# A selective-scan layer: tiles of two states by 64 channels in place of two states by 128 channels side by side

## The reference

```
x1, x2 = layernorm(group_norm(x)) ;  xin = x1 @ W_in_x.T ;  z = x2 @ W_in_z.T       # 384 inner channels
for each direction (forward, backward):
    xc = silu(conv4(xin)) ;  dbl = xc @ W_xproj.T
    dt = softplus(dbl[:12] @ W_dt.T + bias) ;  Bc, Cc = dbl[12:28], dbl[28:44]       # 16 states
    h[d,n] = h[d,n] * exp(dt[d] * A[d,n]) + (dt[d] * xc[d]) * Bc[n]                  # over 3136 pixels
    y[d]   = sum_n h[d,n] * Cc[n] + D[d] * xc[d]
out = ((y_f + y_b) * silu(z)) @ W_out.T + b_out ;  x = x + out
```

## Time and profile before

| | |
|---|---|
| median of 3 runs | 19461.44 us (19454.89 to 19484.83) |
| the profiled execution, span | 19481.1 us |
| PE busy | 17354.2 us (89%) |
| DVE busy | 17262.7 us (89%) |
| POOL busy | 16894.1 us (87%) |
| ACT busy | 13466.7 us (69%) |
| DMA | 2179 MB, 31% of the 16 engines' time |

### The profile page before, as it was taken

The page is one execution under the profiler, slowest core; times in us unless marked ns, Lnnn a source line. Parts: engine busy times, 40 slices in busy tenths (PEclk is TensorE's granted clock), DMA queues, the critical chain, the costliest instruction groups (busy, mean ns, idle before and its releaser), DMA issues. The chain is left out here.

```text
span 19481.1 us, 179917 instructions
## 1 busy us (share of the span) xinstructions
PE 17354.2 (89%) x43808; PEld 7662.4 (39%) x43808; DVE 17262.7 (89%) x13583; ACT 13466.7 (69%) x33829; POOL 16894.1 (87%) x11028
## 2 busy tenths in 40 slices
PE   8989989899898898988989889898998989989898
PEld 3433434334343343433434334343343434434334
DVE  7988989889898898988989899898998989989899
ACT  6767767677676776767767677676776767767676
POOL 6979979799797997979979799797997979979799
PEclk9999999999999999999999999999999999999999
DMA  2313323233231332313323233232332323323233
GB/s 88 139 67 135 140 77 138 68 135 140 78 138 68 135 140 78 138 68 133 140 78 138 68 135 138 80 137 72 139 130 80 140 79 135 123 80 140 81 138 121
DMA packets 531163, 2179.01 MB, mean 112 GB/s; under 512 B 96586, under 2 KB 243684, under 8 KB 529956
## 3 DMA queue, kind: packets, MB, share of 16 engines
q1 hardware_dynamic: 529956, 2166.00, 31.0%
HBM read 1905.48 MB, written 245.63 MB: 110 GB/s over the span
## 5 line engine op out<-in xcount | busy, mean ns | idle before, releaser
L1133 DVE TENSOR_TENSOR_SCAN arena<-ps,arena 128x897 f32<-128x897 f32 x5376 | 10934.7, 2064 | 769.9 <-ACT arena L1287 477.1
L1339 POOL TENSOR_TENSOR arena<-arena 128x896 f32<-128x896 f32 x5376 | 9415.1, 1766 | 625.4 <-PE ps L1041 462.9
L1041 PE MATMUL ps<-arena,ident 128*128 128x448 f32 x21504 | 8997.4, 557 | 892.1 <-POOL arena L1339 889.4
L1271 ACT ACTIVATE ps<-arena,A 128x448 f32<-128x448 f32 x10752 | 6384.6, 626 | 1996.8 <-DVE arena L1133 1963.7
L1041 PEld LDWEIGHTS ps<-arena,ident 128*128 128x128 f32 x21504 | 4039.4, 193 | 5509.2 <-issue 3680.2
L1331 POOL TENSOR_TENSOR arena<-arena 128x896 f32<-128x896 f32 x2688 | 4762.4, 1772 | 84.2 <-DMA arena<-bc_rows 84.2
L1122 DVE TENSOR_TENSOR arena<-ps,arena 128x896 f32<-128x896 f32 x2688 | 2864.3, 1066 | 56.0 <-DMA arena<-bc_rows 56.0
L996 PE MATMUL ps<-arena,diag 128*128 128x448 f32 x5248 | 2087.8, 540 | 2.2
L996 PEld LDWEIGHTS ps<-arena,diag 128*128 128x128 f32 x5248 | 985.9, 189 | 1014.3 <-issue 943.4
L1320 POOL TENSOR_TENSOR arena<-arena 128x448 f32<-128x448 f32 x672 | 653.3, 979 | 512.7 <-DVE arena L1102 512.7
L1035 PE MATMUL ps<-arena,skipd 128*128 128x448 f32 x1344 | 715.9, 616 | 387.2 <-DVE arena L1109 265.6
(11 more groups left out here) (170 smaller groups left out, 19045.8 us busy)
## 6 DMA issues: line engine op xcount, KB each, us to landing
arena<-bc_rows SPq DMA_DIRECT2D x1776, 896.0 KB, 4.6
x_projected<-arena SPq DMA_DIRECT2D x112, 672.0 KB, 3.5
y_forward<-arena SPq DMA_DIRECT2D x112, 672.0 KB, 3.5
arena<-x_projected SPq DMA_DIRECT2D x112, 672.0 KB, 5.7
arena<-y_forward SPq DMA_DIRECT2D x112, 672.0 KB, 4.0
x<-in_x SPq DMA_DIRECT2D x119, 336.0 KB, 3.6
x_normed<-arena SPq DMA_DIRECT2D x112, 336.0 KB, 2.8
arena<-x_normed SPq DMA_DIRECT2D x112, 336.0 KB, 4.6
```

The lines of the kernel that those rows point to most:

```text
L1041: m = e.matmul(y, ident[:, :], pr[:, q % NPR, a * T:a * T + T], start=False, stop=p == NP - 1 and a == 1)
L1133: e.tensor_tensor_scan(rev(hh[:, q % NH, 0:W2], s), rev(decays(q)[:, 0:W2], s), rev(bb[:, q % NB, 0:W2], s), car[:, k, n:n + 1] if i % NC ...
L1271: e.activation(two(decays(q))[:, a, :], dt[:, r % NDT, :], ACT.Exp, scale=Am[s][:, k, 2 * p + a:2 * p + a + 1]).then_inc(c_ex, 1)
L1339: e.tensor_tensor(pr[:, q % NPR, :].rearrange("p (a b) -> p a b", a=2), two(hh[:, q % NH, :]), cr[:, 2 * p:2 * p + 2, :], ALU.mult).then_i ...
```

## The change

A tile still has two halves of 448 columns, but partition `64j + c` now holds state parity j of channel c of a half-block of 64 channels: tile p covers the half-block p % 2 and four states. So:

- `br` and `cr` hold 8 rows a partition in place of 16 (even states on partitions 0 to 63, odd states on 64 to 127), and each load is two transfers onto 64 partitions.
- `dt` and `du` are needed on both partition halves. Side step "dd" spreads `dt` of a block with four transfers of 64 x 448 into `dt2`, and "ud" spreads the lower half of `du` with two into `du2`. Both are in SP's list. The upper half of `du` is spread by a matmul with the new constant `rep` into the PSUM bank DUBANK: "dp" moves from ACT to PE.
- Even tiles' products are POOL's (they read `du2`), odd tiles' DVE's (they read DUBANK).
- PE sums two tiles at once, after the odd one: for each half a of `pr` one matmul of 64 output columns for the even tile (partitions 0 to 63 of YBANK) and one for the odd tile (64 to 127). NPR goes from 3 to 4, `dt` from 6 buffers to 3 and `du` from 4 to 3.

```diff
-ON_VECTOR = [[0, 1, 0, 1, 1, 0, 1, 0]] * 3
+ON_VECTOR = [[0, 1, 0, 1, 0, 1, 0, 1]] * 3
-NB, NH, NPR = 3, 3, 3
-NXC, NDT, NDU = 5, 6, 4
+NB, NH, NPR = 3, 3, 4
+NXC, NDT, NDU, NR2 = 5, 3, 3, 3
...
-        act.append((max(NP * (EJ * i + e) - 2, t + 4.5), "dp", i, e))
+        pe.append((max(NP * (EJ * i + e) - 2, t + 4.5), "dp", i, e))
+        sp.extend([(t + 3.4, "dd", i, e), (t + 5, "ud", i, e)])
...
-            r = PER * i - NP + 2 * G
-            sp.append((max(r + 1, t + 2), "bl", i, G))
-            sp.append((max(r + 3, t + 2.1), "cl", i, G))
+            r = PER * i - NP + 2 * G if i else -100
+            sp.append((max(r + 1, t + 2 + 4 * (G > 0 and not i)), "bl", i, G))
+            sp.append((max(r + 3, t + 2.1 + 4 * (not i)), "cl", i, G))
...
+                if name == "dp":
+                    r = EJ * i + k
+                    freed(w, "cv", 0, 0)
+                    w.wait_ge(c_du, r + 1)
+                    w.wait_ge(c_bv, NV[NP * r])
+                    e.matmul(ps[:, DUBANK, 0:T], rep[64:128, :], du[64:128, r % NDU, :], start=True,
+                             stop=True).then_inc(c_dp, 1)
...
-                w.wait_ge(c_mc, q + 1)
-                for a in range(2):
-                    m = e.matmul(y, ident[:, :], pr[:, q % NPR, a * T:a * T + T], start=False,
-                                 stop=p == NP - 1 and a == 1)
-                m.then_inc(c_sm, 1)
+                if p % 2:
+                    w.wait_ge(c_mc, q + 1)
+                    for a in range(2):
+                        for h in range(2):
+                            m = e.matmul(ps[64 * h:64 * h + 64, YBANK, 0:T], rep[:, 0:64],
+                                         pr[:, (q - 1 + h) % NPR, a * T:a * T + T], start=False,
+                                         stop=p == NP - 1 and a == 1)
...
-            w.wait_ge(c_du, r + 1)
+            spread(w, s_du, 2, r)
...
-                a = 4 * k
-                if not i and not k:
-                    e.dma_start(br[:, 0:2, :], cd[0, 0:2, :].unsqueeze(0).to_broadcast([128, 2, T])).then_inc(s_bf, 16)
-                    a = 2
-                e.dma_start(br[:, a:4 * k + 4, :],
-                            cd[i % 2, a:4 * k + 4, :].unsqueeze(0).to_broadcast([128, 4 * k + 4 - a, T])).then_inc(s_bl[k], 16)
+                for j in range(2):
+                    e.dma_start(br[64 * j:64 * j + 64, 2 * k:2 * k + 2, :],
+                                cd[i % 2, 4 * k + j:4 * k + 4:2, :].unsqueeze(0).to_broadcast([64, 2, T])).then_inc(s_bl[k], 16)
...
+            if name == "dd":
+                r = EJ * i + k
+                freed(w, "t", i, k)
+                w.wait_ge(c_ex, 2 * NP * (r - NR2 + 1))
+                for h in range(2):
+                    for j in range(2):
+                        e.dma_start(dt2[64 * j:64 * j + 64, r % NR2, h, :],
+                                    dt[64 * h:64 * h + 64, r % NDT, :]).then_inc(s_dt[r % NR2], 16)
+            if name == "ud":
+                r = EJ * i + k
+                w.wait_ge(c_du, r + 1)
+                w.wait_ge(c_bp, NP * (r - NR2 + 1) - NV[NP * max(r - NR2 + 1, 0)])
+                for j in range(2):
+                    e.dma_start(du2[64 * j:64 * j + 64, r % NR2, :],
+                                du[0:64, r % NDU, :]).then_inc(s_du[r % NR2], 16)
```

80 lines of the change are left out of this document (43 added, 37 removed).

## The result

The changed kernel takes 20785.56 us (median of 4 runs, 20745.35 to 20805.15) against 19471.43 us (4 runs, 19454.89 to 19484.83) before: ratio 1.067, 95% interval 1.0657 to 1.0684. It is 6.7% slower. The prediction was 19245 us, between 18900 and 19560, and faster. It was wrong in sign and outside its range. The profiled execution of after has a span of 20743.6 us, 1262.5 us more than that of before.

A forecast was written before the change was run, and what follows sets the result against it. PE, full in stretches, was taken as the bound, with POOL and DVE busy times as floors. Forward 13.0 plus backward 10.5 minus start 10 gave 13.5 us an image, 216 for 16: 19481 to 19265, median 19245 us, range 18900 to 19560.

The forecast's parts named there:

- ud: Transfers spreading `du` at chunk borders: there 2.8 us after `du`; POOL waits 0.5 us a backward chunk, hidden forward.
- The time of an issue: SP's issue queue: one transfer issued every 0.47 us or so.
- Landing: SP's transfers: a 112 KB transfer lands 2.2 us after its issue.
- The start: Layer 1's start, once per image: first scan 9.6 to 15.6 us late, 12.5 taken, 2.5 back, net 10 us.
- The sign named for it: Layer 1's start: the prediction would be wrong if the start cost more than 16 us.
- Side by side: Sums on PE: two instructions share one slot; slots fall from 159 to 117 forward, 168 to 126 backward.
- The excursion: PE going from 128 columns to 64 and back: 0.24 us each, at most 2.9 us a chunk, in free time.
- That rival: Sums on PE: pairs don't run in parallel, PE stays full, no steady gain; 19620 us, chance 0.05.
- Backward: Layer 1's backward chunks: 2.0 us gained out of 3.7, less 0.5 us of POOL's wait; 10.5 us an image.
- Forward: Layer 1's forward chunks: 2.0 us gained out of 3.1, DVE's 3.38 us stall below 1 us; 13.0 us an image.
- The falling clock: PE's clock falls behind longer idle gaps: 3 us a backward chunk, forward even; about 19960 us, chance 0.13.
- The slower case: Whole kernel: slower than before by more than 0.2%, 39 us; chance 0.23.

The follow-up runs named there:

- e1_ud_first: The changed kernel with one due time moved: the spread of a chunk's first `du` goes on SP right behind its first `dt` spread; 19441.23 us, ratio 0.9991.
- e2_wide: e1_ud_first with each sum matmul at 128 output columns again, zero weights for the other half, so none run in parallel; 19959.68 us, ratio 1.0258.
- e7_alt: The kernel before with only the table of products changed to strict alternation between DVE and POOL; 19544.57 us, ratio 1.0037.
- e4_pairs: The kernel before with only sums two tiles at a time, full width, four output buffers, one fewer for `dt` and `du`; 19778.12 us, ratio 1.0161.
- e5_cv_late: e1_ud_first with a forward chunk's second convolution, and the steps reading it, due two tiles later, behind the block's last sums; 19065.86 us, ratio 0.9789.

## Why the prediction was wrong, point by point

**"ud" was the step that failed.** It was costed as `du` + issue + landing = 2.8 us, with 0 to 1.3 us a backward border, nothing forward and "and more if SP's queue is still moving" as an aside. The sum has to walk SP's list: twelve transfers stand ahead of "ud" at every border, from the block's own "dd" on. Of POOL's 1494.2 us of waits 16 x 18.9 = 303 are the starts; the other 1191 us are 13 borders in each of 16 images, 5.7 us each, forward and backward, and e1_ud_first takes it away by order alone. At 13 x 5.7 = 74 us an image this is nearly the whole loss of 79. The prediction printed SP's order for the start only, not for a border, and it is the border that comes 13 times an image.

**The time of an issue was undersized.** 0.47 us was taken from loads onto 128 partitions, and there nine transfers have eight steps between them, so 4.23 / 8 = 0.53. Onto 64 partitions it is 0.61 to 0.69. The twelve at the border are 7.7 us and not 5.6. The trace of the kernel before has the very shape of the spreads, in layer 0, two in 1.19 us:

```profile
91.84 1.19 SPq L858 DMA_DIRECT2D arena<-arena  x2
```

**Landing was undersized.** 2.2 us from layer 0; at the border 3.7 us passed, and over the kernel the median is 3.1. From the pages, the packets of before and of after, and after's DMA issues inside SBUF with KB each and us to landing:

```profile
DMA packets 531163, 2179.01 MB, mean 112 GB/s; under 512 B 96586, under 2 KB 243684, under 8 KB 529956
DMA packets 1109659, 1820.18 MB, mean 88 GB/s; under 512 B 189530, under 2 KB 1053556, under 8 KB 1108404
...
arena<-arena SPq DMA_DIRECT2D x4160, 112.0 KB, 3.1
```

**The start**: 9.6 to 15.6 us late, 12.5 taken; it was 17.6. The slower bound of the rate was right (231 GB/s, measured 229), and "ud" needed its own time behind it. Of the 2.5 us that were to come back a part did: the eighth scan of the first image starts 292.74 - 271.76 = 21.0 us behind the first, before 23.0, and in the mean of 16 images it is 21.5 and 22.8.

```profile
292.74 2.03 DVE L1151 TENSOR_TENSOR_SCAN arena<-ps,arena 128x897 f32<-128x897 f32 x1 [0.45 <-POOL arena L1354]
```

That chunk 1 is longer by 3.8 all the same comes at its end, at the border: from its first to its last scan it is 68.9 us in after and 68.8 before. The sign named for it (over 16 us) was met; the other one (first scan of the first image at 271 to 277 us) looked right at 271.76 only because that image reached layer 1 seven us earlier ("td" ends at 249.92, before at 256.91).

**Side by side was right.** Eight sum instructions take 1.72 us where eight took 3.17, four slots of 0.376 us and a little. PE is still busy 60.7 and 56.4 us of a chunk and not 47 to 50, since part of it runs at the lower clock (0.80 and 0.93) and since the profile's busy time lies above the slots to begin with (64.66 us for 59.8 before). The excursion in e1_ud_first costs what was taken, 0.24 us: 504.41 - (501.31 + 3.01) = 0.09 on the way in and (506.06 - 504.41) - 1.50 = 0.15 by the end of the way out. Backward it is hidden, as POOL is at its floor. That rival is excluded; a kernel in which they don't run side by side is e2_wide.

**Backward was right once SP was in order.** 2.0 us were to go before the cost of spreads, at most 3.7; 71.1 - 68.2 = 2.9 went, spreads included: a border's wait is 0.2 us in most backward chunks of e1_ud_first, the 0.2 us that the prediction worked out before its allowance for SP's queue. The 1.7 us left for POOL and DVE getting in each other's way was too careful: in a backward chunk of e1_ud_first (68.24 us) POOL is busy 67.55 us and DVE 66.73.

**Forward was wrong in place.** The stall behind the read-out was to shrink below 1 us; in e1_ud_first it is 3.19. The estimate of 12.3 us for the chain against 12 us of need put the margin at zero and still booked 2.0 us of gain. What it left out: the table, which leaves DVE less to do while ACT waits (e7_alt, +1.1 us); the sums in twos ahead of the second convolution (e4_pairs, +3.6); and that ACT waits for the convolution itself, ahead of the read-out, in order. With the convolution and its readers moved, 70.1 - 68.0 = 2.1 us are gained, the size that was forecast.

**The falling clock** was a rival at 0.13 with the wrong half: it was priced at 3 us a backward chunk and nothing a forward one. It costs nothing that shows backward (68.2 us, POOL's floor, at a mean of 0.87 and 0.90 in a chunk of e1_ud_first and of e5_cv_late) and 1.9 us a forward chunk, where it sits behind one gap. The mean told little: e2_wide has 0.955 and is slower.

**The slower case itself** was given 0.23, 0.13 of it for the clock. No rival was built on SP's order, though the rows on SP were there.
